# A scan kernel whose B and C rows are spread by DMA from HBM, with B*u on GpSimd and decay and state in PSUM halves

## The reference

```
x = x + L0(groupnorm(x))      # 7x7 depthwise convolution, its weights made from the image itself
x = x + L1(groupnorm(x))      # three selective scans at 1024, 256 and 64 positions, both directions

def _ssm(x, xw, dtw, dtb, Al, Dv, g, be):             # 128 channels, 16 states
    xd = einsum('bdl,kd->blk', x, xw)                 # 8 dt rows, 16 B rows, 16 C rows
    delta = softplus(einsum('blr,dr->bld', dts, dtw) + dtb)
    A = -exp(Al)
    dA  = exp(delta[..., None] * A)                   # the decay, one per channel, state and position
    dBx = delta[..., None] * Bs[:, :, None, :] * xt[..., None]
    def step(h, inp):
        h = h * da + dbx                              # the scan
        return (h, einsum('bdn,bn->bd', h, c))        # times C, summed over the states
    y = ys + xt * Dv
    return _layernorm(y, g, be)
```

## Time and profile before

| what | value |
|---|---|
| median of three runs | 4848.01 us |
| profiled execution, its span | 4848.26 us, 4846.5 us |
| PE busy | 3681.5 us (76%) in 14924 matmuls |
| DVE busy | 4213.7 us (87%) in 3384 |
| ACT busy | 2496.6 us (52%) in 5590 |
| POOL busy | 2320.7 us (48%) in 1412 |
| mean granted TensorE clock | 0.860 of full speed |
| DMA | 39.62 MB, mean 8 GB/s |

### The profile page before, as it was taken

The page is one execution under the profiler, slowest core; times in us unless marked ns, Lnnn a source line. Parts: engine busy times, 40 slices in busy tenths (PEclk is TensorE's granted clock), DMA queues, the critical chain, the costliest instruction groups (busy, mean ns, idle before and its releaser), DMA issues. The chain is left out here.

```text
span 4846.5 us, 47836 instructions
## 1 busy us (share of the span) xinstructions
PE 3681.5 (76%) x14924; PEld 1645.5 (34%) x14924; DVE 4213.7 (87%) x3384; ACT 2496.6 (52%) x5590; POOL 2320.7 (48%) x1412
## 2 busy tenths in 40 slices
PE   6878787778877777787778877778787778877734
PEld 4433333333333333333333333333333333332300
DVE  2299988988999899988988999898989988899798
ACT  4454655445455554555445465554556445454432
POOL 0064543645445364543635445364543635446374
PEclk8999888888988889898888989889898988888855
DMA  1000000000000000000000000000000000000000
GB/s 37 1 9 1 19 1 18 1 1 19 1 18 1 1 19 1 19 1 18 1 1 19 1 18 1 1 19 1 18 1 18 1 1 19 1 9 1 9 0 9
DMA packets 12287, 39.62 MB, mean 8 GB/s; under 512 B 1728, under 2 KB 3280, under 8 KB 11984
## 3 DMA queue, kind: packets, MB, share of 16 engines
q1 hardware_dynamic: 11984, 35.90, 2.0%
HBM read 19.11 MB, written 16.78 MB: 7 GB/s over the span
## 5 line engine op out<-in xcount | busy, mean ns | idle before, releaser
L748 PE MATMUL pconv<-pad,diag 128*128 128x512 f16 x8064 | 2104.9, 415 | 103.2 <-ACT diag L1053 64.6
L1295 POOL TENSOR_TENSOR y<-y,work 128x1024 f32<-128x1024 f32 (+2 forms) x672 | 1331.4, 1981 | 1671.9 <-DVE work L510 1657.0
L1148 ACT ACTIVATE work<-delta,nega 128x1024 f32<-128x1024 f32 (+1 forms) x768 | 695.1, 929 | 1522.4 <-DVE work L500 1314.0
L748 PEld LDWEIGHTS pconv<-pad,diag 128*128 128x128 f16 x8064 | 831.9, 104 | 1279.0 <-issue 330.7
L500 DVE TENSOR_TENSOR_SCAN work<-work,slot_b 128x1024 f32<-128x1024 f32 x496 | 1131.8, 2282 | 27.3 <-issue 0.4
L799 PE MATMUL slot_b<-bcs,sel 96*128 96x512 bf16 (+2 forms) x1536 | 421.4, 380 | 657.6 <-DVE work L500 413.6
L478 DVE TENSOR_TENSOR slot_b<-slot_b,u 128x1024 f32<-128x1024 f32 x496 | 608.1, 1226 | 225.1 <-PE slot_b L799 206.9
L1290 POOL TENSOR_TENSOR work<-work 128x512 f32<-128x512 f32 (+3 forms) x384 | 547.8, 1427 | 227.2 <-DVE work L513 209.7
L510 DVE TENSOR_TENSOR work<-slot_c,work 128x1024 f32<-128x1024 f32 x512 | 626.8, 1224 | 22.2
L799 PE MATMUL slot_c<-bcs,sel 96*128 96x512 bf16 (+2 forms) x1536 | 416.3, 376 | 269.2 <-DVE work L510 179.6
L799 PEld LDWEIGHTS slot_b<-bcs,sel 96*128 96x128 bf16 x1536 | 113.3, 107 | 896.9 <-DVE work L500 574.7
(11 more groups left out here) (175 smaller groups left out, 3838.1 us busy)
## 6 DMA issues: line engine op xcount, KB each, us to landing
xr<-in_x SPq DMA_DIRECT2D x16, 1024.0 KB, 4.8
out<-ob SPq DMA_DIRECT2D x16, 1024.0 KB
w<-in_w SPq DMA_DIRECT2D x2, 256.0 KB
wc<-in_wc SPq DMA_DIRECT2D x2, 256.0 KB
wbc<-in_wbc SPq DMA_DIRECT2D x1, 144.0 KB
win<-in_win SPq DMA_DIRECT2D x1, 128.0 KB
wz<-in_wz SPq DMA_DIRECT2D x1, 128.0 KB
wo<-in_wo SPq DMA_DIRECT2D x1, 128.0 KB
```

What stands on the lines that cost most here:

```text
L748: ins = nc.tensor.matmul(bank(pconv, k), w, pad[:, t, part, rows:rows + 16, dx:dx + W], start=first and m == 0, stop=last and m == 2)
L1148: ins = nc.scalar.activation(o, delta[:, so:so + ln], ACT.Exp, scale=nega[:, st, n0 + n:n0 + n + 1])
L1295: pool.tensor_tensor(yv, yv, src[:, 0] if len(src.shape) == 3 else src, ALU.add).then_inc(q_y.sem, 1)
```

## The change

What it does, part by part:

- PE spreads nothing. ACT copies each chunk's 32 B and C rows from PSUM to `rows` as floats, SP writes them to a scratch in HBM (`bc_rows`), and SP reads back, for each unit, 4 KB of B and 4 KB of C with a source that repeats for all 128 partitions: two DMAs of 128x1024 floats, 512 KB each as written into SBUF. B has two buffers (`bb`), C three (`cb`).
- The three bf16 parts and what made them go: `rest`, its DVE subtraction (441), ACT's second copy (1120) and POOL's subtraction (1253).
- B*u moves from DVE to POOL (`inputs`), ahead of the gathers; a unit's gather is done one unit later than before.
- The decay is written to `slot_b` and the scan's result to `slot_c`, both PSUM, in halves (banks) of 512 columns. A half of the decay of unit k+1 can be written only when the scan of unit k has read that half. A scan of 1024 becomes two of 512, the second starting from the last column of the first; a unit at the 256-position level becomes scans of 256. The product by C is made in halves too.
- DVE's order: a half's product by C comes after the next half's scan.
- ACT makes half 0 of the decay of unit k+1 where it made the decay of unit k+2, and half 1 at the end of its unit k, behind all else.
- What PE projected into `slot_b` in the bridge goes to `pm`.

The core of the diff:

```diff
+            def get_rows(i, k, row0, dst, done):
+                lv, st, dd, n0, m = UNITS[k]
+                ln = LEVEL[lv][0]
+                o = ROWS_AT[{3: 0, 2: 1, 1: 2 if dd == 0 else 4}[lv]][0] + (row0 + n0) * ln
+                sp.dma_start(dst, bc[None, o:o + m * ln].to_broadcast([P, m * ln])).then_inc(done.sem, 16)
+            def get_b(i, k):
...
+                if k >= BR:
+                    sp.wait_ge(u_bx.sem, u_bx.at(i, k - BR + 1))
+                get_rows(i, k, 0, bb[:, k % BR, :], b_in[k % BR])
+            def get_c(i, k):
+                if k >= CR:
+                    sp.wait_ge(q_pr.sem, q_pr.at(i, weighed(products_of(k - CR)[-1])))
+                get_rows(i, k, NS, cb[:, k % CR, :], c_in[k % CR])
...
-                nc.vector.tensor_tensor(rest[:, k, 0:n], bank(pm, 0)[0:64, 0:n], bcs[0:64, s:s + n], ALU.subtract).then_inc(ch_rest.sem, 1)
-                nc.vector.tensor_tensor(o, i0, i1, ALU.mult).then_inc(u_bx.sem, 1)
...
+            def scan(i, q, p):
...
+                n = min(ln, HALF)
+                for o in range(b * HALF, (b + 1) * HALF, n):
+                    hv, av, bv = slot_c[:, o:o + n], slot_b[:, o:o + n], bx[:, k % 2, o:o + n]
+                    if d:
+                        hv, av, bv = hv[:, ::-1], av[:, ::-1], bv[:, ::-1]
+                    ins = nc.vector.tensor_tensor_scan(hv, av, bv, start, ALU.mult, ALU.add)
+                ins.then_inc(q_h.sem, 1)
...
+                nc.vector.tensor_tensor(half(h[:, q % HR], b), bank(slot_c, b), half(cb[:, k % CR], b), ALU.mult).then_inc(q_pr.sem, 1)
...
-            def spread(i, k, slot, row0, done):
...
+                b = decay_banks(k)[p]
                 if k >= 2:
+                    act.wait_ge(q_h.sem, q_h.at(i, last_half(k - 1, b) + 1))
+                w = min(ln, HALF)
+                for o in range(b * HALF, (b + 1) * HALF, w):
+                    n, c = divmod(o, ln)
+                    ins = nc.scalar.activation(slot_b[:, o:o + w], delta[:, so + c:so + c + w], ACT.Exp,
+                                               scale=nega[:, st, n0 + n:n0 + n + 1])
...
-                    if k + 2 < NU:
-                        decay(i, k + 2)
+                    if 1 <= k < NU - 1:
+                        decay(i, k + 1, 0)
...
+                if i is not None and 1 <= k < NU - 1:
+                    decay(i, k + 1, 1)
                 if j is not None and k == PREP + 3:
                     copy_f(j, 0)
...
+            def inputs(i, k):
...
+                pool.wait_ge(b_in[k % BR].sem, b_in[k % BR].at(i, 16 * (k // BR + 1)))
+                if k >= 3:
+                    pool.wait_ge(q_h.sem, q_h.at(i, half_at(*halves_of(k - 2)[-1]) + 1))
+                    ins = pool.tensor_tensor(bx[:, k % 2, :], bb[:, k % BR, :], us, ALU.mult)
...
-                    for q in products_of(k):
-                        gather(i, q)
+                    if k + 1 < NU:
+                        inputs(i, k + 1)
+                    for v in (k - 1, k) if k == NU - 1 else (k - 1,):
+                        for q in products_of(v):
+                            gather(i, q)
```

More of the change, by code:

```diff
@@ L54, with banks, halves_of, half_at @@
 NN = len(NORMS)
-CONSTS = ["ident", "cen", "ones", "grp", "grp_m2", "half", "half_m2"]
+CONSTS = ["ident", "cen", "ones", "grp", "grp_m2", "halves", "halves_m2"]
 def products_of(u):
     return [q for q, (v, _) in enumerate(PRODUCTS) if v == u]
-def build(nc, a, out):
+def banks(q):
+    u, d = PRODUCTS[q]
+    return (1, 0) if UNITS[u][0] == 1 and d else (0, 1)
+def halves_of(u):
+    return [(q, p) for q in products_of(u) for p in (0, 1)]
+def half_at(q, p):
+    return 2 * (q - 2) + p
+def last_half(u, b):
+    return max(half_at(q, p) for q, p in halves_of(u) if banks(q)[p] == b)
+def decay_banks(u):
+    return banks(products_of(u)[0])
+def weighed(q):
+    return q + 1 if q < 2 else 2 * q
+NHALF = 2 * (NP - 2)
+HALF_BANK = [banks(q)[p] for q in range(2, NP) for p in (0, 1)]
+def build(nc, a, bc, out):
     with ExitStack() as ctx:
@@ L162, in build @@
         sz = sb("sz", [P, HW])
-        bcs = sb("bcs", [96, LS], BF16)
-        rest = sb("rest", [64, 2, HALF])
+        rows = sb("rows", [2 * NS, 2, HALF])
         delta = sb("delta", [P, LS])
@@ new lines, in bridge @@
+            def bridge(i, j, m):
+                if j is not None:
+                    put_rows(j, 0)
+                    put_rows(j, 1)
+                    if i is not None:
+                        sp.wait_ge(u_bx.sem, u_bx.at(j, 0))
+                        sp.sem_inc(sp_held, 1)
+                        sp.wait_ge(q_pr.sem, q_pr.at(j, 0))
+                        sp.sem_inc(sp_held, 1)
+                    for k in range(2):
+                        get_b(j, k)
+                        get_c(j, k)
+                if i is not None:
+                    sp.wait_ge(ob_ready.sem, ob_ready.at(i + 1, 0))
+                    sp.dma_start(ov[i], ob[:, :, :]).then_inc(ob_free.sem, 16)
@@ L337, in _ @@
+            stages(unit, bridge, sp)
             sp.wait_ge(ob_free.sem, ob_free.at(B + 1, 0))
@@ L602, in unit @@
                 if i is not None:
[L603 to L612 removed]
+                    products(i, k)
+                    if k in CHUNK_FIRST:
+                        chunk_first(i, CHUNK_FIRST[k])
                     if k in CHUNK_LAST:
```

310 lines of the change are left out of this document (143 added, 167 removed).

## The result

The changed kernel takes **4727.37 us** (median; 4724.41 to 4728.14), against 4848.01 before: the ratio is 0.9746, with a 95% interval of 0.9724 to 0.9768. Forecast were 4620 us and a range of 4440 to 5150. The gain is about half of the 230 us expected.

A forecast was written before the change was run, and what follows sets the result against it. DVE bounds the kernel, POOL next: a turn of 210 + 36.2 + 30 = 276.2 against 292.6 us, 16.4 less, 230 over 14 turns, so 4848.3 - 230 = 4618, say 4620 us; range 4440 to 5150.

The forecast's parts named there:

- POOL then sets the pace: In 1024-position units POOL needs 4.72 us per unit, against DVE's 3.8 plus odd jobs.
- the last two images: Images of 249.9 and 246.2 us without another image's rows or weights: no change, give or take 10 us each.
- DVE released by POOL's product: Sign of being right: DVE idle before scans until POOL's product, and until ACT's decay half in units 34 to 36.
- the tail grew, the bridge shrank: Units 33 to 36 go from 28.3 to 36.2 us; the bridge from 35.9 to 30 us.
- ACT's rows held by a slower PE: Sign of being wrong: PE falls to the lower clock level and holds ACT's row waits.
- Rival 1, the broadcast: 16 DMA engines reading one 4 KB row become the bound; 5310 us at 2.5 times the load's price; chance 0.16.
- Both waits are met some us before they matter: SP's in-order list of B and C copies, each behind its wait, doesn't delay their use.
- Rival 2, late decays: Single `slot_b` leaves late decays unabsorbed: T33 (POOL's end of unit 33's product) 232 us, turn 298, 4925 us; chance 0.18.
- 9 us of stalls: Stalls where ACT or DVE is late: unit 6's half 1 of the decay and others, 9 us per turn.
- The step that failed: the port: Shared SBUF port costs POOL 10 us up to unit 33, and DVE 0.7 us before `conv_add` in the tail.
- The base: One turn of 292.6 us, 14 of them plus 249.9 us for the next-to-last image giving 4346.5.
- The own range: Stalls and port from 10 to 35 us per turn, tail 30 to 42: 4450 to 4800 us.

The follow-up runs named there:

- experiment 4: Changed kernel with B*u moved back from POOL to DVE: 4888.21 us, ratio 1.0074.
- experiment 8: Kernel with both halves of all decays made early (4545 us), POOL adding only 512 of 1024 columns to y: 4358.24 us, ratio 0.8995.
- Experiment 5: Changed kernel whose copies of B and C bring only 128 of 1024 columns from unit 5 on: 4729.11 us, ratio 0.9746.
- experiment 6: Changed kernel with two landing buffers for C in place of three: 4803.53 us, ratio 0.9902.
- experiment 3: Changed kernel with the second half of the next unit's decay made early in units 1 to 32 alone: 4584.03 us, ratio 0.9449.
- Experiment 9: Changed kernel with the norms of units 30 and 33 keeping their product in PSUM, nothing else: 4620.18 us, ratio 0.9527.
- experiment 7: Changed kernel with decays in one SBUF buffer instead of PSUM, and two landing buffers for C: 5651.47 us, ratio 1.1686.
- experiment 11: Fastest full-result kernel (early decays, reordered tail, norms in PSUM; 4390.55 us) with row 2 of diagonals also made in the bridge: 4420.26 us, ratio 0.9113.

## Why the prediction was half right

**The direction and the bounds.** That DVE's list shrinks was right, and experiment 4 shows that moving B*u is the whole gain. That POOL then sets the pace was right where nothing else holds DVE: in the last two images (experiment 8). In a turn of the changed kernel it is not so. DVE's waits in units 5 to 32 (2571.85 to 2736.87 us):

```profile
DVE slot_c L572 <- ACT slot_b L1190: 22.9, 7, 5.9
...
DVE slot_c L572 <- POOL bx L1334: 1.0, 3, 0.5
```

The prediction had named DVE released by POOL's product there as a sign of being right. The parts that cost were forecast: the tail grew, the bridge shrank. One sign of being wrong, ACT's rows held by a slower PE, did not come: they waited 2.9 us for PE in the whole span (L1087), at a granted clock of 0.80 in the mean.

**Rival 1, the broadcast.** It falls. The copies of a unit come to 1.05 MB, and 661 MB took 41.1% of 16 engines' 4726 us; per MB that is the price in the earlier trace rows (11.5% of 25 us for 1.05 MB is 2.9 us; 0.411 x 4726 / 630 is 3.1 us). Experiment 5 settles it. The case had one soft spot that wasn't seen: SP's order. "Both waits are met some us before they matter" holds with three buffers for C, and fails with two (experiment 6). "Both" has an exception at units 1 to 4, where POOL waits 39.0 us for B in the whole span.

**Rival 2, late decays.** Its mechanism is real, at the size that the forecast had counted already. The forecast put 9 us of stalls into units 0 to 32, and experiment 3 took 10.1 us out of a turn; this term was right. The rival wanted 16 us more.

**The step that failed: the port.** It was priced as "POOL loses the like", 10 us of POOL's time, and 0.7 us in the norm ahead of `conv_add`. The exclusive lock was the right picture, but the sum charged the wrong engine. A held operation of POOL loses a short DVE operation (the longest add took 3.24 us): its adds and products of 1024 columns have a median of 2.35 us and means of 2.40 and 2.37, 2 us per image in all. A held DVE operation waits out what is left of 2.35 us, and the next can be held again: 23 us per image (experiment 4). POOL paid for that by waiting for DVE.

The window from 2523.55 to 2736.87 us lasted 213.3 us, forecast were 210. POOL was busy 178.3 us in it; forecast were 181.9; unit 0's two trees, for one, took 3.85 and 2.95 us where 5.85 each were taken from the earlier trace rows. Idle it was 35.1 us, forecast 27.8 with the port's 10 and the first 5.8 included. Its largest waits in that window:

```profile
POOL y L1362 <- DVE h L581: 13.5, 6, 3.8
POOL delta L1302 <- DVE rs L530: 6.4, 4, 3.0
POOL h L1357 <- DVE h L551: 5.6, 1, 5.6
POOL bx L1334 <- DVE slot_c L572: 5.2, 3, 2.0
```

DVE pays in the tail too. Unit 33 of DVE in the changed kernel:

```profile
2740.60 0.68 DVE L625 TENSOR_TENSOR rs<-pm,rs 128x512 f32<-128x512 f32 x1
2741.32 1.67 DVE L637 TENSOR_SCALAR o<-rs,vec,bes 128x512 f32<-128x512 f32 x1
2743.02 2.78 DVE L610 TENSOR_TENSOR o<-o 128x256 f32<-128x256 f32 x2
2745.93 1.28 DVE L506 SCALAR_TENSOR_TENSOR xn<-pconv,csc,xn 128x1024 f32<-128x1024 f32 x1
```

The norm takes 5.2 us where 3.1 (2.4 and 0.7) were taken, so `conv_add` ends 10.3 us into the unit instead of 8.2. That is 2.1 of the tail's 2.9 us, for half 1 of the decays of units 34, 35 and 36 then came 2.0 to 2.1 us behind the forecast. Experiment 9 shows it as a cause: with two norms off the port a turn is 6.6 us shorter, of 7.6 by which the forecast was short. It does not prove that the missing time is just this, since it also takes away one instruction per norm that was in the forecast at its old price (0.95 us).

**The base, and the last two images.** The prediction took one turn of 292.6 us for the mean and found it borne out, since 14 of them and 249.9 us end at the last image. But 249.9 was no reading of its own: by the scans shown above the next-to-last image lasts 269.7 us and the 14 turns 291.2 in the mean. From 291.2 down to 276.2 the turns would have given 210 us, not 230; they gave 103.9. The last two images were to give nothing, give or take 10 us each; they gave 12.7 and 5.5. The base made the forecast 20 us too low and these two images made it 18 us too high; that they cancel in the total is luck. What is left is the 7.6 us of every turn, 106 us. The next-to-last image was also taken to be free of rows; those of the last image from the fifth on are made there (ACT is busy 123.3 us, in the last image 81.5), and with early decays in the middle it falls from 257.0 to 249.9.

**The own range.** 4450 to 4800 moves stalls and port alone. With the tail's 30 to 42 us moved too, as its words say, the same sum gives 4364 to 4882.

## What to carry to other kernels

When work moves to POOL, price what it does to DVE's other instructions and not to POOL's: here those with all operands in SBUF, off the path until then, went to two or three times their time, and one operand left in PSUM freed them. When a buffer goes from double to single, move its producer to the head of the producing engine's list in the same edit; here that was worth 182 us, more than the 121 of the change. Mark turns by the same instruction in both kernels, and read every image's length instead of working it out from one turn. A queue in order passes the wait of one buffer on to the next transfer, so a buffer is only spare if nobody stands behind it.

## What the runs showed of the hardware

- A scan of 512 columns with both inputs in SBUF and a POOL operation on SBUF exclude each other: beside a busy POOL the scans take 2.09 to 2.43 us in the mean, with one input in PSUM 1.23 to 1.30; POOL's 1024-column operations go from 2.37 to 2.66 and from 2.40 to 2.96 (experiment 7).
- Short DVE operations on SBUF can be held for most of an operation of POOL: `rs<-rs,es` of 512 columns took 0.69 us at one place and 2.72 at another in the same turn of experiment 11.
- One 4 KB row copied to 128 partitions (512 KB) lands in 4.1 to 4.6 us in the median, two of them per unit, with the 16 engines at 41% over the span.
- ACT writes the decays' half to PSUM in 0.685 us, to SBUF in 0.717 (experiment 7).
